# A twelve-stage decoder on one core: fetching the first tiles' rows before the second tile's weights, and summing expert outputs by TensorE

## The reference

```python
def _L0_ffn_ref(x, w_up, w_down, b_up, b_down, w_router):      # 8 experts, 2 picked
    logits = einsum('bsd,ed->bse', x, w_router)
    top_vals, top_idx = top_k(logits, 2)
    router_weights = softmax(top_vals)
    up = einsum('eud,bsd->bseu', w_up, x) + b_up
    down = einsum('edu,bseu->bsed', w_down, gelu(up)) + b_down
    sel = take_along_axis(down, top_idx[..., None], axis=2)
    return einsum('bskd,bsk->bsd', sel, router_weights)

def _L1_ffn_ref(x, gate_w, gate_b, w1, b1, w2, b2):            # 8 experts
    scores = softmax(x @ gate_w + gate_b); topk_s, topk_i = top_k(scores, 2)
    wf = dispatch of topk_s to the 8 experts                    # the picked score, else 0
    for i in range(8):
        y = relu(xf * wf[:, i] @ w1[i] + b1[i]) @ w2[i] + b2[i]
        out = where(wf[:, i] > 0, y, out)                       # the last picked expert wins
    return out

x = layernorm(x + _L0_ffn_ref(x, ...))
x = layernorm(x + _L1_ffn_ref(x, ...))
```

## Time and profile before

| | us |
|---|---|
| median of 3 runs (lowest to highest) | 1737.9 (1737.52 to 1742.2) |
| the profiled execution's own time | 1745.63 |
| its span | 1743.8 |
| TensorE busy | 1557.0 (89% of the span) |
| VectorE busy | 910.1 (52%) |
| ScalarE busy | 678.8 (39%) |
| GpSimd busy | 412.5 (24%) |

### The profile page before, as it was taken

One profiled execution on the slowest core, in us unless ns is written; L12 is line 12 of the kernel. 1 busy time (PEld: TensorE's weight loads), 2 busy tenths in 40 slices (PEclk: granted clock), 3 DMA queues, 4 the chain that ended last, 5 costly groups with the idle time before them and its releaser, 6 DMA issues.

```text
span 1743.8 us, 40008 instructions
## 1 busy us (share of the span) xinstructions
PE 1557.0 (89%) x14902; PEld 1287.8 (74%) x14902; DVE 910.1 (52%) x2316; ACT 678.8 (39%) x1611; POOL 412.5 (24%) x627
## 2 busy tenths in 40 slices
PE   7998998789995889998699599997998999999998
PEld 6876776678994667776588477775786776789897
DVE  3665777521105557778311364567344555566764
ACT  3334776322333236654122323662663444211110
POOL 2224776510004331111100134552111111000101
PEclk9998999999997999999899799998999999999999
DMA  5443000188971002110578201101002100033232
GB/s 206 150 155 136 29 27 17 52 294 290 323 250 49 2 1 83 30 29 12 214 281 297 88 1 46 42 27 49 2 1 69 35 29 2 25 121 98 91 105 68
DMA packets 41852, 166.76 MB, mean 96 GB/s; under 512 B 5984, under 2 KB 16864, under 8 KB 30176
## 3 DMA queue, kind: packets, MB, share of 16 engines
q1 hardware_dynamic: 39392, 159.14, 26.3%
q0 software_dynamic: 2304, 5.51, 1.0%
HBM read 140.22 MB, written 24.41 MB: 94 GB/s over the span
## 4 chain that ended last, share of the span: by engine, by line
PE 69%; DVE 13%; issue 8%; DMA 3%; POOL 3%; ACT 2%; SPq 1%; DVEq 0%; POOLq 0%; ACTq 0%
PE bank L1996 6%; PE bank L2009 6%; PE bank L1389 4%; PE bank L1938 4%; PE bank L1940 4%; PE bank L1939 4%; PE bank L1376 3%; PE bank L857 2%; PE bank L866 2%; DMA xrow<-slots 2%; PE bank L831 2%; PE bank L958 2%; PE bank L1403 1%; PE bank L1364 1%; PE bank L1359 1%
## 5 line engine op out<-in xcount | busy, mean ns | idle before, releaser
L3664 POOL TENSOR_TENSOR mv<-mv,cst 112x1 f32<-112x1 f32 x88 | 20.7, 235 | 583.1 <-DVE mv L2684 583.1
L2603 ACT ACTIVATE htile<-bank,wup 128x128 f32<-128x128 f32 x280 | 79.9, 369 | 190.1 <-PE bank L1996 190.1
L2378 ACT ACTIVATE arena<-big,nm 112x375 f32<-112x375 f32 x256 | 143.7, 605 | 23.4 <-DVE nm L3348 14.4
L1389 PEld LDWEIGHTS bank<-cst,arena 112*125 112x125 f32 x768 | 100.8, 197 | 44.6 <-issue 22.0
L1996 PE MATMUL bank<-xtile,wup 128*128 128x128 f32 x1120 | 133.0, 278 | 0.3 <-DVE xtile L3511 0.2
L1996 PEld LDWEIGHTS bank<-xtile,wup 128*128 128x128 f32 x1120 | 130.0, 194 | 1.0 <-DVE xtile L3511 0.9
L3527 DVE COPY yrow<-bank 128x256 f32<-128x256 f32 x35 | 14.9, 425 | 217.6 <-PE bank L2009 217.6
L2009 PE MATMUL bank<-wdn,htile 128*128 128x256 f32 x560 | 126.3, 379 | 0.0
L1389 PE MATMUL bank<-cst,arena 112*125 112x112 f32 x768 | 116.0, 290 | 8.4 <-POOL arena L3838 4.7
L2009 PEld LDWEIGHTS bank<-wdn,htile 128*128 128x128 f32 x560 | 103.9, 190 | 12.7
L3838 POOL TENSOR_SCALAR arena<-arena,c_lo 112x375 f32<-112x375 f32 x64 | 98.2, 1547 | 37.1 <-ACT c_lo L2382 37.0
(11 more groups left out here) (386 smaller groups left out, 3728.4 us busy)
## 6 DMA issues: line engine op xcount, KB each, us to landing
wup<-in_moe_up SPq DMA_DIRECT2D x35, 1028.0 KB, 7.3
wdn<-in_moe_dn SPq DMA_DIRECT2D x35, 1024.0 KB, 6.0
vspace<-in_ring SPq DMA_DIRECT2D x40, 512.0 KB, 3.9
ctxs<-parts SPq DMA_DIRECT2D x30, 564.0 KB, 3.9
slots<-mlpw SPq DMA_DIRECT2D x11, 1024.0 KB, 6.4
parts<-ctxs SPq DMA_DIRECT2D x8, 564.0 KB, 3.1
xrow<-slots SPq DMA_DIRECT2D x35, 128.0 KB, 5.1
slots<-yrow SPq DMA_DIRECT2D x35, 128.0 KB, 7.0
```

The source lines that it names most:

```text
L1389: mm = pe.transpose(bank[4 + (3 * g + t) % 2][0:KT, j * T:(j + 1) * T], c_pr[:, g, j, t * KT:(t + 1) * KT], ident[0:T, 0:T])
L2378: nc.scalar.activation(c_pr[:, g, j, :], c_sc[:, g % 2, j, :], ACT.Exp, bias=nm[:, p, h:h + 1], scale=-1.0).then_inc(cexp_done, 1)
L2603: ins = nc.scalar.activation(htile[:, g % 2, m, :], bank[2 + 2 * (g % 2) + m // 4][:, m % 4 * ROWS:(m % 4 + 1) * ROWS], func, bias=wup[:, ...
```

## The change

It has two parts. In SP's program, the wait for the scatters and the fetch of rows 0 come straight after registers 0, and rows 1 straight after registers 1, ahead of the weights of tile 1; rows 2 stay behind those weights. In the end of the expert layers, TensorE sums the picked outputs and acc into a bank (6 or 7, by t modulo 2), multiplying with a diagonal of the routing weights (`mix`, L0_ffn) or with the identity; VectorE makes the diagonals during the loop over tiles, and takes the statistics and the normalised rows straight from the bank. The sums on VectorE are gone.

```diff
-    Ffn("L0_ffn", dn=8),
+    Ffn("L0_ffn", dn=16),
...
-    Ffn("L1_ffn", dn=8),
+    Ffn("L1_ffn", dn=16),
...
             xs = take(T, B, DM)
+            mix = xs.rearrange("p b n -> p (b n)")[:, 0:2 * B * T].rearrange("p (k t n) -> p k t n", k=2, t=B)
...
                 registers(0)
+                sp.wait_ge(sent, 16 * B * sum(PICKS[:n + 1]))
+                rows_to(0)
                 registers(1)
+                rows_to(1)
                 up_weights(1)
                 down_weights(1)
                 registers(2)
-                sp.wait_ge(sent, 16 * B * sum(PICKS[:n + 1]))
-                rows_to(0)
-                rows_to(1)
                 rows_to(2)
                 up_weights(2)
                 down_weights(2)
...
+                def outputs(t):
+
+                    pe.wait_ge(got_in[t % 4], 16 * (2 * sum(PICKS[:n]) + PICKS[n] * (t // 4 + 1)))
+                    if t >= 2:
+                        pe.wait_ge(xln_ready, at(sub, "row", t - 2, 1))
+                    parts = [(mix[:, k, t, :] if n == 0 else ident[0:T, 0:T], ygot[:, t, k, :]) for k in range(PICKS[n])]
+                    parts.append((ident[0:T, 0:T], acc[:, t, :]))
+                    for k, (picks, rows) in enumerate(parts):
+                        mm = pe.matmul(bank[6 + t % 2][0:T, 0:DM], picks, rows, start=(k == 0), stop=(k == PICKS[n]))
+                    mm.then_inc(dn_ready, 1)
+
+                pe.wait_ge(edn_done, tile_of(n, count - 1) + 1)
+                pe.wait_ge(dn_done, db + B)
+                outputs(0)
+                outputs(1)
                 for t in range(B):
                     if t >= B - 2:
                         for _ in range(3):
                             warm(bank[3], 256)
                     rows_t(sub, t, t % 2, bank[t % 2])
+                    if t + 2 < B:
+                        outputs(t + 2)
                     opening(sub, t)
...
                     if i < B:
+                        for k in range(2 if n == 0 else 0):
+                            dve.tensor_scalar(mix[:, k, i, :], c("ident", T)[:, 0:T], gw[:, 1 + k, i:i + 1], None, ALU.mult)
                         dve.wait_ge(dn_ready, db + i + 1)
...
-                mixed = Steps(dve, mix_step, 0, B)
+                def sums(t):
+
+                    return bank[6 + t % 2][0:T, 0:DM]
+
+                def stats_of(t):
+
+                    v = START + 3 * (sub.base["ln"] + t)
+                    dve.wait_ge(dn_ready, db + B + t + 1)
+                    dve.bn_stats(st[:, t % 2, :], sums(t)).then_inc(ln_dve, 2)
+                    dve.wait_ge(ln_dve, v + 2)
+                    apart(dve)
+                    dve.bn_aggr(mv[:, t % 2, 0:2], st[:, t % 2, :]).then_inc(ln_dve, 1)
+
+                def rows_of(t):
+
+                    dve.wait_ge(xt_ready, xt_at(sub, t) - 2)
+                    dve.wait_ge(xres_done, at(sub, "row", t, -1))
+                    dve.wait_ge(ln_pool, START + 2 * (sub.base["ln"] + t) + 2)
+                    dve.tensor_scalar(xln[:, t % 2, :], sums(t), mv[:, t % 2, 0:1], mv[:, t % 2, 3:4], ALU.subtract, ALU.mult)\
+                        .then_inc(xln_ready, 1)
+
                 for t in range(B):
-                    if t >= 2:
-                        dve.wait_ge(xln_ready, at(sub, "row", t - 2, 1))
-                        apart(dve)
-                    dve.wait_ge(got_in[t % 4], 16 * (2 * sum(PICKS[:n]) + PICKS[n] * (t // 4 + 1)))
-                    if n == 0:
-                        mixed(dve.scalar_tensor_tensor(out=acc[:, t, :], in0=ygot[:, t, 0, :], scalar=gw[:, 1, t:t + 1],
-                                                       in1=acc[:, t, :], op0=ALU.mult, op1=ALU.add))
-                        ins = dve.scalar_tensor_tensor(out=res[:, t % 2, :], in0=ygot[:, t, 1, :], scalar=gw[:, 2, t:t + 1],
-                                                       in1=acc[:, t, :], op0=ALU.mult, op1=ALU.add)
-                    else:
-                        ins = dve.tensor_tensor(res[:, t % 2, :], ygot[:, t, 0, :], acc[:, t, :], ALU.add)
-                    ins.then_inc(ln_dve, 1)
-                    stats(sub, t, t % 2, 0)
+                    stats_of(t)
                     if t:
                         inverse(t - 1)
-                        rows_out(sub, t - 1, (t - 1) % 2)
+                        rows_of(t - 1)
                     opening(sub, t)
                 inverse(B - 1)
-                rows_out(sub, B - 1, 1)
+                rows_of(B - 1)
+                dve.sem_inc(dn_done, B)
```

More of the change, by code:

```diff
@@ L492, in decoder @@
         v_zero = sem("v_zero")
-        mix_step = sem("mix_step")
         rt_ready, rt_step, rt_exp = sem("rt_ready"), [sem("rt_step0"), sem("rt_step1")], sem("rt_exp")
```

## The result

| | before | after |
|---|---|---|
| time, median | 1741.76 us (20 runs, 1735.17 to 1751.57) | 1754.95 us (20 runs, 1748.72 to 1766.68) |
| profiled execution | 1745.6 us, span 1743.8 | 1754.65 us, span 1752.9 |

The ratio of the times is 1.0087, 95% interval 1.0072 to 1.0103: 15.1 us slower, between 12.5 and 17.9 (the two medians by themselves lie 13.2 us apart). The two profiled executions differ by 9.1 us only: the four stages that the change touches are 14.2 us longer in after's, and the rest of that execution is about 5 us shorter. For each expert layer I take two stretches of the timeline: **start and loop**, from the issue of the last scatter (`slots`) to VectorE's copy of the last tile's outputs (`yrow`), and **end**, from there to ScalarE's copy of row 7 (`x_res<-xln`). "Four stages" is the sum of the four against before's.

A forecast was written before the change was run, and what follows sets the result against it. TensorE was taken to carry most of the chain of waits, VectorE setting the pace in the ends. Ends +11.3 and +10.6, starts -0.9 and -5.2, sum to +15.8 us: 1737.9 becomes 1753.7, range 1741 to 1766.

The forecast's parts named there:

- Every row makes one full round: In both ends, each row passes TensorE and VectorE with nothing overlapped; ends +11.3 us in L0_ffn, +10.6 in L1_ffn.
- Size of a round: In the ends, time per row: 4.66 us at low and 3.16 at full clock in L0_ffn, 3.8 and 2.7 in L1_ffn.
- The clock: In both ends, TensorE stays at low clock until the next layer's queries and keys follow outputs(5), then full clock.
- rival B: In the ends, full clock comes early: net +2 us, 1740, if throughout; partly, up to +10; chance 0.18.
- a clock of 1.00 before 545: In L0_ffn's end, full TensorE clock before 545 us on the trace was listed as showing the prediction wrong.
- Start of L0_ffn: Tile 0 starts 2.3 us sooner, then TensorE waits 1.4 for rows 2; gain 0.9 us, bounds 0 and 2.3.
- Start of L1_ffn: Tile 0 starts at 857.0 instead of 862.38, with earlier row fetches; gain 5.2 us, bounds 4 and 6.
- Diagonals at nothing: In the loop, VectorE's 16 scalings, 0.2 to 0.4 us each, are covered by its idle time: 0.
- The sum: Over both starts and both ends: 11.3 + 10.6 - 0.9 - 5.2 = +15.8 us.
- Rival D: In the ends, matmuls cost a quarter of the fillers' price, 0.22 us at low clock: -2 us, 1736; chance 0.06.
- Rival C: In the ends, low clock lasts to the end of both: +21 and +14, net +29 us, 1767; chance 0.10.
- Rival E: Rounds in the ends overlap in an unseen way and both starts gain in full, 8 us: 1730; chance 0.04.

The follow-up runs named there:

- e6_row_at_once: The after kernel with VectorE normalising row t directly behind its own statistics instead of behind those of row t+1; 1740.41 us, ratio 1.0011.
- e5_three_banks: The after kernel with a third bank for the sums, so that outputs(t+3), not outputs(t+2), waits for row t; 1737.74 us, ratio 0.9984.
- e11_fillers_in_wait: The after kernel with five filler matmuls on TensorE in the wait for rows 2 of L0_ffn; 1754.83 us, ratio 1.0078.
- e1_start_only: The before kernel with SP's new order alone in both expert layers, sums left on VectorE; 1737.62 us, ratio 0.9984.
- e8_three_banks_rows_first: The after kernel with three banks for the sums and rows 0, 1 and 2 ahead of tile 1's weights; 1734.36 us, ratio 0.9969.
- e4_rows_first: The before kernel with rows 0, 1 and 2 all fetched ahead of tile 1's weights, sums left on VectorE; 1735.05 us, ratio 0.9978.

## Why the prediction was right, and which of its steps were not

The forecast was 1753.7 us; 1754.95 was measured. As a difference it was +15.8 us against +15.1 by the ratio and +13.2 by the medians. The forecast's own mechanism decides the result, but two terms of the sum were off by several microseconds in opposite directions, and that it came out this close is luck.

- **Every row makes one full round.** Shown. e6_row_at_once undoes only the order on VectorE and e5_three_banks only the limit of two banks, and either brings both ends back to within 3 us of before.
- **Size of a round.** Forecast 4.66 and 3.16 us in L0 at low and full clock, 3.8 and 2.7 in L1; measured 4.88 and 3.39 in L0, 4.02 and 2.96 in L1. The matmuls were priced right: the six instructions take 549.93 to 552.70 = 2.77 us, as rows 9 have it. Statistics to transposes took 1.58 us instead of 1.45; the 0.13 is the normalised row, 0.54 us read from the bank against 0.41 from `res`. Smaller hops around the matmuls make up the other 0.1. Today's 2.1 us a row in L1 was 2.0.
- **The clock.** "I take low until the 16 instructions of the next layer's queries and keys": right in L1_ffn (full clock forecast from 1003.6, measured from 1004.4; row 3 ready at 998.5 and 999.3, row 6 at 1009.1 and 1010.5), so that end cost 12.2 us against 10.6 forecast. In both ends the forecast lets queries and keys end 0.2 us sooner than its own terms add up to. **This step failed in L0_ffn.** There rival B held in the profiled execution: full clock from 536.8, an end that cost 4.9 instead of 11.3. It is also one of the prediction's own signs of being wrong, "a clock of 1.00 before 545". The row brought up for low clock, TensorE busy 13.54 of 17.0 us at 0.50, doesn't carry: 19.16 of 26 us went at full clock in after, and in e11_fillers_in_wait 18.80 of 30.7 at low clock, in the same code. The busy share of a stretch of pieces did not tell the clock. e11's end, +13.0, is the kind that I had forecast, with +11.3.
- **Start of L0_ffn.** The wait for rows 2 was foreseen, 1.4 us; it was 2.44: tile 0's up started 0.4 us sooner behind the last scatter than forecast, and rows 2 landed 0.7 later, 0.5 of which is the step with registers between rows 0 and rows 1, 2.10 us (356.76 to 358.86) and not 1.6. The forecast gain of 0.9 became a loss of 1.4 by tile 0's down. **The step that failed**: the forecast read its gain at the start of tile 1's up and left that up at the 3.57 us of before, with nothing for the clock; behind the wait the clock fell and it took 5.20. e11_fillers_in_wait shows it directly, with 3.57 once the wait is filled. The other 1.2 us of the 2.7 arose further down the loop of that one profile, where TensorE waited three times, 1.9 us in all, for rows (after 400); e1_start_only, with the same start, has no such wait there.
- **Start of L1_ffn.** Forecast 5.2, measured 4.7 by tile 0's down and 5.6 by the last tile. The way there differed: tile 0's up started 0.8 us sooner than forecast and took 5.13 us instead of 5.84, since the clock rose during it, but then TensorE waited 2.11 us for rows 2, which the forecast had landing in time.
- **Diagonals at nothing.** Right: 16 of them, 0.27 us each, and the trace shows nobody who waited for one. Line 3538 of after: count, duration least, median and most in ns, first and last start.

```profile
L3538 DVE TENSOR_SCALAR arena<-cst,arena x16: 268/270/274, 369.2 to 427.0; 112x112 f32<-112x112 f32 x16
```

- **The sum.** Forecast -0.9, -5.2, +11.3, +10.6 = +15.8; the stages gave +2.7, -5.6, +4.9, +12.2 = +14.2. L0's start was 3.6 too good and its end 6.4 too bad: the closeness of the total is owed in part to these two. Single executions of after range over 18 us, but those of before over 16, so how often the long kind of L0's end comes can't be read from that.
- **Rival D** (matmuls at a quarter of the fillers' price) falls: leaving one out shortened a round by 0.85 us at low clock, two instructions of 0.43. The Trainium skill (TensorE: Matmul & The Clock Gate, "Back-to-back issue gap") gives 262 cycles for 256 columns, at 1.2 GHz an estimate of 0.22 us for a matmul, a quarter of that; for these f32 products the trace disagrees. **Rival C** (low clock to the end of both) was not seen: clock 1.00 from 1004.4 on in L1_ffn, and from 562.7 even in e11's long end of L0_ffn. **Rival E** falls with the 2.44 us wait.

## What to carry to other kernels

When sums move to an idle engine, first write down who waits for whom in each row and with how many buffers: two banks and a reader that runs one row behind left nothing to overlap, and either a third bank or a reader without that lag cured it, with the same operations. A transfer pulled forward helps only if everything that its consumer needs next is pulled forward too; here 128 KB left behind 2 MB made a wait, and the matmuls after it ran at low clock unless the wait was filled. With those 128 KB in front too, the weights themselves came about 1 us late. Where single profiles differ by more than the change is worth, compare stages, and take the total from many runs.

## What the runs showed that I had not expected

- VectorE's `TENSOR_SCALAR`, 112x256 f32, took 0.54 us from a bank and 0.41 from a tile, the statistics 0.43 from either.
- The same end of L0_ffn ran at full clock after 6.8 us (after) or only after 30.7 us (e11_fillers_in_wait), with the rows 3.39 or 4.88 us apart: 8.1 us between two executions of the same instructions.
- 20 fillers ahead of the end of L1_ffn gave full clock for less than two rounds; it fell again at 993.4. In L0_ffn of after, with one matmul more in each round, it stayed full to the end. What keeps it up was not settled.
- A wait of 1.13 us (e8_three_banks_rows_first, start of L0_ffn) was followed by low clock, one of 0.90 us in the same place (e4_rows_first) was not.
